# Decoder layer on one core: attention rounds written out, the first FFN weight units prepared earlier, the hand-over to the mixer rearranged

## What is computed

```python
x = x + attention(layernorm(x))      # 16 heads of 32, causal softmax, biases
x = x + mixer(ctx, ctx, layernorm(x))  # 32 heads of 8: all 8x8 products k_i * v_j along the
                                       # sequence, causally convolved with the head's kernel, + D,
                                       # then summed against q_i
x = x + ffn(layernorm(x))            # rows and weights rounded to int8 grids; gate and up of 1408
                                       # (w_gate_up: 2816 rows), silu(gate) * up, down to 512
```

## Time and profile before

| | us |
|---|---|
| median of 3 runs | 1222.92 (1220.35 to 1227.15) |
| the profiled execution | 1222.95 |
| its span | 1221.1 |
| PE busy | 1130.7 (93%) |
| DVE busy | 1002.1 (82%) |
| POOL busy | 945.4 (77%) |
| ACT busy | 878.4 (72%) |

### The profile page before, as it was taken

How to read it: one execution, slowest core, us unless ns; L and a number is a source line. 1 busy time by engine, 2 the same in 40 slices (tenths; PEclk the granted TensorE clock), 3 DMA queues, 4 the chain that set the end, 5 groups by cost and what they waited for, 6 DMA issues and landing times. The chain is left out here.

```text
span 1221.1 us, 31917 instructions
## 1 busy us (share of the span) xinstructions
PE 1130.7 (93%) x10114; PEld 814.0 (67%) x10114; DVE 1002.1 (82%) x3147; ACT 878.4 (72%) x1811; POOL 945.4 (77%) x1085
## 2 busy tenths in 40 slices
PE   7889999999999999998768899999999999999996
PEld 6777777878777787776446566666666666666662
DVE  5678888878787887887768788988889888898875
ACT  3878878878787887887746566667666676666764
POOL 0377787767778776877736799999999999999983
PEclk9989999999999999999679999999999999999999
DMA  6345655556555555566675433444434443344410
GB/s 213 101 165 183 187 169 159 186 168 194 181 167 169 166 174 185 180 207 191 235 230 190 146 105 129 137 147 137 115 127 137 148 137 114 129 137 148 134 32 26
DMA packets 88342, 188.84 MB, mean 155 GB/s; under 512 B 12351, under 2 KB 29017, under 8 KB 88089
## 3 DMA queue, kind: packets, MB, share of 16 engines
q1 hardware_dynamic: 87353, 186.74, 48.7%
q10 hardware_dynamic: 864, 0.66, 0.3%
HBM read 107.57 MB, written 54.62 MB: 133 GB/s over the span
## 5 line engine op out<-in xcount | busy, mean ns | idle before, releaser
L780 ACT ACTIVATE prob<-masked,negmax 128x128 f32<-128x128 f32 (+1 forms) x512 | 206.4, 454 | 73.6 <-DVE negmax L915 72.6
L915 DVE CUSTOM_DVE_ANT_0 masked<-s_ps,mask_f 128x128 f32<-128x128 f32 (+1 forms) x512 | 161.1, 352 | 29.7 <-PE s_ps L661 14.9
L1255 PE MATMUL f_ps<-wqkv,xiT 128*128 128x512 bf16 (+1 forms) x768 | 174.5, 364 | 2.4 <-DVE up L1712 1.5
L1538 POOL TENSOR_TENSOR tree<-prod 128x512 f32<-128x512 f32 x128 | 163.1, 1274 | 10.6 <-DVE prod L1642 10.4
L1446 ACT ACTIVATE silu<-gate,sx 128x512 f32<-128x512 f32 (+1 forms) x96 | 66.0, 687 | 136.1 <-DVE gate L1706 136.1
L539 POOL TENSOR_TENSOR kv_s<-kv_f,kv_s 128x1152 f16<-128x1152 f32 x64 | 152.3, 2379 | 4.6 <-ACT kv_s L794 4.6
L921 DVE TENSOR_TENSOR pT_lo<-t_ps,pT_hi 128x384 f16<-128x384 f32 x256 | 140.6, 550 | 15.4 <-ACT pT_hi L788 15.1
L532 POOL TENSOR_TENSOR kv_f<-c_in 128x1024 f32<-128x1024 f32 x64 | 146.0, 2281 | 0.2 <-DMA c_in<-in_ctxr 0.2
L788 ACT CAST pT_hi<-t_ps 128x384 f16<-128x384 f32 x256 | 122.2, 478 | 29.7 <-PE t_ps L670 28.5
L598 PE MATMUL g_ps<-x_all,wqkv 128*128 128x256 f16 x512 | 140.1, 274 | 3.1 <-DVE x_all L879 3.1
L599 PE MATMUL g_ps<-x_all,wqkv 128*128 128x256 f16 x512 | 140.1, 274 | 0.0
(11 more groups left out here) (187 smaller groups left out, 3591.9 us busy)
## 6 DMA issues: line engine op xcount, KB each, us to landing
kv_pairs<-kv_s SPq DMA_DIRECT2D x64, 576.0 KB, 3.4
kv<-kv_pairs SPq DMA_DIRECT2D x32, 1152.0 KB, 8.6
c_in<-in_ctxr SPq DMA_DIRECT2D x64, 192.0 KB, 2.5
q_st<-w_raw SPq DMA_DIRECT2D x192, 64.0 KB, 2.0
k_st<-w_raw SPq DMA_DIRECT2D x192, 64.0 KB, 2.0
x_all<-in_x SPq DMA_DIRECT2D x16, 512.0 KB, 6.6
x_res<-in_x SPq DMA_DIRECT2D x16, 512.0 KB, 6.1
x_after_attention<-x_out SPq DMA_DIRECT2D x16, 512.0 KB, 4.4
```

The lines of the kernel that those rows point to most:

```text
L780: ins = nc.scalar.activation(prob[h % 2][:, at:at + w], masked[h % 2][:, at:at + w], ACT.Exp, bias=negmax[:, h % 2, t:t + 1], scale=-1.0)
L915: ins = nc.vector.tensor_tensor_reduce(masked[h % 2][:, at:at + w], s_ps[h % 2][:, at:at + w], mask_f[:, S - w:S], -1.0, FAR, ALU.add, ALU ...
L1255: mm = nc.tensor.matmul(f_ps[side][:, 0:w], xiT[:, t, :], w1T[:, t, side * I_FF + at:side * I_FF + at + w], start=t == 0, stop=t == DT - 1)
L1538: nc.gpsimd.tensor_tensor(tree4[:], pr[:, :, 0:4 * w], pr[:, :, 4 * w:8 * w], ALU.add).then_inc(t4_done, 1)
```

## The change

All rounds of attention are written out: the `Fori` of each of the five engines becomes a Python loop, and the branches for register values go. Pair sets are numbered through (`q`), and their number per round comes from `pair_sets(i)`, which is 4 for all.

Units 0 to 3 are loaded at the end of SP's lists for rounds 8 and 9, their maxima found one half at a time in steps 3 and 6 of rounds 10 to 13 (one unit a round), their scales in step 7, the halves rounded in steps 8 and 11. Round 15 has no unit work. Units 4 and 5 are loaded in round 14, 6 and 7 early in round 15.

In round 15 POOL's list has a pair set, a low part and a value bias ahead of the residual's bias; ACT makes the high part of the set before at step 5 instead of 3. In the tail POOL adds the last residual's bias ahead of the last two low parts. PE turns the four halves of units 0 and 1 before the last "A" jobs, into banks that the heads leave free; ACT and DVE take two each. DVE handles units 4 and 5 before the first "O" job's end and unit 6 between the two. The last `x_out` is stored by halves of 128 tokens: the mixer's first loads need the first half alone.

At the mixer's start `FIRST` has six halves instead of ten, and DVE finds maxima and scales of all four units 7 to 10 after its first statistics, where it found those of 7 and 8 before them.

```diff
+UNIT_MAX = {(B - 6 + u, s): (u, k) for u in range(4) for s, k in ((3, 0), (6, 1))}
+UNIT_SCALES = {(r, s + 1): u for (r, s), (u, k) in UNIT_MAX.items() if k == 1}
+UNIT_SCALE = {(r, s + 2 + 3 * n): (u, n) for (r, s), (u, k) in UNIT_MAX.items() if k == 1 for n in range(2)}
...
+    def find_part(self, dve, u, k):
+
+        if k == 0:
+            dve.wait_ge(self.loaded[u], 16)
+        n = UNITS[u][1] + k
+        ins = self.nc.vector.tensor_reduce(self.maxima[:, n:n + 1], self.home(u)[:, k, :], AX_X, ALU.max, apply_absolute_value=True)
+        if k == 1:
+            ins.then_inc(self.max_done, 1)
...
+    def scale_part(self, act, u, k):
+
+        if k == 0:
+            act.wait_ge(self.inv_done, u + 1)
+        n, rows = UNITS[u][1] + k, self.home(u)[:, k, :]
+        ins = self.nc.scalar.activation(rows, rows, ACT.Copy, bias=MAGIC, scale=self.inv[:, n:n + 1])
+        if k == 1:
+            ins.then_inc(self.scaled, 1)
...
+                if i == B - 8:
 
                     sp.wait_ge(w_split, split_after(3))
                     W.load(sp, 0, w1)
                     W.load(sp, 1, w1)
-                if last:
+                if i == B - 7:
+                    W.load(sp, 2, w1)
+                    W.load(sp, 3, w1)
+                if i == B - 2:
 
                     for j in range(HPT):
                         sp.wait_ge(stacked[j], (B - 1) * (6 * 16))
                     W.load(sp, 4, w1)
                     W.load(sp, 5, w1)
...
-            with sp.Fori(LOOP0, LOOP1 - 1, 2) as i:
+            for i in range(LOOP0, LOOP1, 2):
                 body(i, 0)
                 body(i + 1, 1)
...
-            store_pairs(B - 1, 2)
-            store_pairs(B - 1, 3)
-            store(B - 1, jobs_before(B) + len(JOBS_END))
+            store_pairs(NQ - 2)
+            store_pairs(NQ - 1)
+            for m, done in ((0, x_stored), (1, x_last)):
+
+                sp.wait_ge(g_free, jobs_before(B) + 3 + m)
+                sp.dma_start(x1d[B - 1, m * P:(m + 1) * P, :], x_out[:, m, :]).then_inc(done, 16)
+            sp.wait_ge(early_taken, EARLY)
...
+                if last:
+
+                    pairs(q)
+                    pairs_low(q - 1)
+                    value_bias(i, p, 0)
+                    biased_residual()
+                    pairs(q + 1)
+                    pairs_low(q)
+                    value_bias(i, p, 1)
+                    pairs(q + 2)
+                    pairs_low(q + 1)
+                    value_bias(i, p, 2)
+                    pairs(q + 3)
+                    return
...
             value_bias(B - 1, 1, HPT - 1)
-            pairs_low(B - 1, 3)
             pool.wait_ge(res_loaded, B * 16)
             nc.gpsimd.tensor_tensor(x_res[:], x_res[:], bo_b[:, None, :].broadcast_to([P, TT, D]),
                                     ALU.add).then_inc(res_biased, 1)
+            pairs_low(NQ - 2)
+            pairs_low(NQ - 1)
...
+            pe.wait_ge(max_done, B * H)
+            pe.wait_ge(plo_done, B * H)
+            for k in range(EARLY):
+                W.turn_rows(pe, *early[k], early_bank[k], eye_f).then_inc(early_turned, 1)
...
-                if k == 2:
-                    for u in range(IN_ROUND, IN_TAIL):
-                        W.find_maxima(dve, u)
-                        W.find_scales(dve, u)
+                for u in {2: range(IN_ROUND, IN_TAIL - 1), 3: range(IN_TAIL - 1, IN_TAIL)}.get(k, ()):
+                    W.find_maxima(dve, u)
+                    W.find_scales(dve, u)
                 low(B, 0, n0 + k, j, g_ps[(n0 + k) % G], h0 + his(JOBS_END, k))
...
+    FIRST = HALVES[EARLY:10] + ["T"]
+    FIRST_BANK, FIRST_ACT = (0, 1, 2, 3, 4, 5, 0), (0, 2, 4)
...
-            for u in (7, 8):
-                W.find_maxima(dve, u)
-                W.find_scales(dve, u)
+            take(1)
+            take(3)
             ln_stats(0, 0)
             aggregate(0, st2, st2_done, mv2, mv2_done)
-            take(2)
-            take(4)
-            for u in (9, 10):
+            take(5)
+            for u in (7, 8, 9, 10):
                 W.find_maxima(dve, u)
                 W.find_scales(dve, u)
             take(6)
-            take(8)
-            take(10)
```

More of the change, by code:

```diff
@@ L550, in body, with biased_residual @@
             def body(i, p):
-                jobs = round_jobs(i)
-                first = isinstance(i, int) and i == 0
-                if has(jobs, "O"):
-                    value_bias(i - 1, 1 - p, HPT - 1)
+                jobs, n, q, last = round_jobs(i), pair_sets(i), pairs_before(i), i == B - 1
+                def biased_residual():
                     pool.wait_ge(res_loaded, i * 16)
@@ L732, in _ @@
                 body(i, i % 2)
-            with pe.Fori(LOOP0, LOOP1 - 1, 2) as i:
+            for i in range(LOOP0, LOOP1, 2):
                 body(i, 0)
@@ L854, in _ @@
                 prob_high((B - 1) * H + s - 2, s - 2)
-            pairs_high(B - 1, 3)
+            pairs_high(NQ - 1)
+            for k in range(0, EARLY, 2):
+                act.wait_ge(early_turned, k + 1)
+                u, b, nb = early[k]
+                nc.scalar.activation(W.target(u, b, nb), early_bank[k][:, 0:nb * P].rearrange("p (t c) -> p t c", t=nb), ACT.Copy,
+                                     bias=-MAGIC).then_inc(early_taken, 1)
             n0 = jobs_before(B)
```

205 lines of the change are left out of this document (113 added, 92 removed).

## The result

| | before | after |
|---|---|---|
| median, us | 1222.92 (7 runs, 1220.35 to 1227.15) | 1215.6 (7 runs, 1212.2 to 1219.7) |
| ratio | 1 | 0.9939, 95% 0.9920 to 0.9959 |
| profiled execution / span | 1222.95 / 1221.1 | 1219.47 / 1217.7 |

The change makes the kernel 0.6% faster, 7.3 us by the medians, where 12 had been forecast. A ratio interval that ends at 0.9959 excludes no change at all, but leaves the size open between 0.4% and 0.8%.

The account below looks back on a forecast made before the run. PE was taken to set a full round's length, with loop edges and round 15's mutual waits on top. From 1222.95 us, -9.2 + 2.4 + 0.5 - 7.5 + 0.5 + 1.2 = -12.1 gave 1211 us, range 1203 to 1220.

Parts of the forecast that it names:

- Loop edges: Even rounds after a loop edge: writing the loop out removes the edges, -9.2 us (bounds 0 and 9.2).
- Rival 5: Loop written out: the edges' time stays as fetch waits in straight-line code, 1220.2 us; chance 0.06.
- Units in rounds 10 to 13: Weight units 0 to 3 put into these rounds make PE late by +0.6 us a round, +2.4 in all.
- their loads: Unit loads ahead of the residual's load in rounds 8 and 9: POOL late but catches up, +0.5 us.
- a push on step 9: Rounds 10 to 13: second half maximum, small ops and step 8 rounding delay step 9's row maximum about 0.6 us, step 12 too.
- The rounding of step 11: Rounds 10 to 13, ScalarE: hidden behind steps where PE bounds; if that cover is gone, 0.66 us a round.
- Rival 3: Rounds 10 to 13, step 7: POOL's op blocks VectorE's small scaling, up to 2.1 us a round, 1219.4 us; chance 0.07.
- Round 15: Without unit work VectorE and ScalarE stop delaying each other: -7.5 us (bounds 2 to 11).
- Tail: Last value bias V to the mixer's first x load: POOL's reordered list takes what the halves give, +0.5 us (-2.5 to +3).
- the halves: Tail: storing the last x by halves frees the first x load from the second's landing, 1 to 2 us less.
- Mixer start: Four units behind the first statistics: +3.0 for units 7 and 8, less about 1.8 for evictions, +1.2 us.
- signs: Right: rounds 4-9 35.0, 10-13 35.3-36, round 15 28-31 us. Wrong: 2 us scaling in 10-13, round 15 above 34.

Follow-up runs that it names:

- unroll_only: The kernel before with its five loops written out and nothing else; 1214.69 us, ratio 0.9922.
- queue_order: Kernel after with loads of units 4 to 10 behind round 15's second pair store and its residual ahead of the x store; 1214.85 us, ratio 0.9893.
- all_four: All repairs on the kernel after: units 0-3 spread over rounds 6-14, weights requeued, earlier maxima, low parts first, scalings by column, unit 6 later; 1200.68 us, ratio 0.9795.
- maxima_first: Kernel after with maxima and scales of units 7 and 8 ahead of the mixer's first evictions and statistics on VectorE; 1214.45 us, ratio 0.9899.
- loads_behind: Kernel after with the loads of units 0 to 3 behind the residual's load on SyncE's queue instead of ahead; 1213.11 us, ratio 0.9897.

## Why the prediction was right, and where its sum was not

The direction was right and the time (1215.6) lies in the range of 1203 to 1220, just outside the forecast's own 1207 to 1215; the forecast of 1211 was 4.6 us too low. It was right by the loop alone: all other terms were forecast at -2.9 in sum, and against the kernel with the loop alone their stages come to +0.8. Their errors go both ways (units and loads 4.9 too cheap, the tail 2.1 too dear), and that these partly cancel is luck.

From profile to profile, up to the products, the stages are: rounds 0 and 1 -0.9 (not forecast; +0.8 with the loop alone, so not an effect that can be relied on), rounds 2 to 13 -1.7, round 15 to V -5.4, V to x load -1.6, from there to the statistics +0.2, statistics to products +1.4, together -8.0.

- **Loop edges, -9.2.** Right: -9.4 with the loop alone, and the "issue" waits that remain, 0.9 us at most, are hidden. Rival 5 is out: no round keeps the edge's time.
- **Units in rounds 10 to 13, +2.4, and their loads, +0.5.** These are the terms that failed: +7.8 against the loop alone. The working priced the second half maximum by a push on step 9 that would reach step 12. That push isn't there: steps 9 and 12 kept their 2.02 and 1.61 us. What it missed was nearer: the divide of step 7, on the same engine and in the same step, for which the values waited (+0.44). The rounding of step 11, called hidden, cost 0.54; its named fallback, 0.66 if that cover is gone, was the better figure. Together 1.1 a round, 4.5 in all.
- The loads: "POOL works 26.8 of 35 us, so it catches up" was true of POOL, but not of what meets a late POOL: 1.5 us by lateness itself and 1.9 by the blocked scaling in round 10 (1.2 and 2.1 by the estimate above). Round 9 paid next to nothing (35.10). Rival 3 had mechanism and price right (2.07 us, the 2.1 forecast) and the number of places wrong: one round of four in the kernel after, since it takes a late POOL to bring them together. It deserved to be a part of the loads' term, not a separate case.
- **Round 15, -7.5.** -5.4 from profile to profile up to V, -4.7 from first to last scores, -7.8 against unroll_only, of which about 2 are that run's own held-up scaling. The mechanism was as stated (the maxima's wait 8.2 to 1.9). The prediction counted the small scaling's 3.8 us as work and didn't see that 3.1 us of it were the wait of its rival 3, met already in the kernel before. What was not seen is that ScalarE's wait for its pair buffer, 3.7 us, would follow from the weights on the queue ahead of a store; in the kernel before it was 2.2 us up to V, a row that the prediction didn't read. In the two kernels without it (queue_order, all_four) the gain is 9.7 to 9.8.
- **Tail, +0.5.** -1.6 measured. The chain named there (residual, bias, low parts, last pair store, x halves) is what the runs show, 10.6 us from the bias; it was sized 0.8 us too dear behind the bias (V + 4 to V + 15.4 is 11.4), and the bias began at V + 2.7, not V + 4. That the halves give 1 to 2 was too much: 0.66.
- **Mixer start, +1.2.** +1.4 measured, and +2.1 against unroll_only; maxima_first takes 3.0 off, the forecast's own 3.0 for units 7 and 8.

What was written as signs came out as: rounds 4 to 9 at 34.9 to 35.2 and no "issue" wait of 2.4 us (right), rounds 11 to 13 at 36.06, just above the 36 given, round 10 outside, round 15 at 32.1 from first to last scores where 28 to 31 stood, the last pair store at V + 9.8 where "after 10 us" stood. A scaling of 2 us in rounds 10 to 13, a sign of being wrong, was there once.

## What to carry to other kernels

Work moved off a crowded stage fits elsewhere only in pieces that are no larger than one idle gap of the engine that gets it: list, step by step, which instruction stands behind it on that engine and who waits for that one. A load that is added to a queue is paid by what stands behind it there, so put transfers with a long due time behind the short-dated ones of the same place. And a change whose parts cancel hides both: the loop alone gave all of this one's gain, and the rest of it, rearranged after each part had been measured by itself, became worth another 1.3% (0.9795 against 0.9922).

## What the runs showed of the hardware

- A small VectorE scaling on 128x2 f32 that begins inside a GpSimd op lasts until that op ends (2.07, 2.08, 2.35 us beside ops on 128x1024 or 128x1152, 0.39 beside one on 128x128). In the thirteen profiles it did so with more than 0.17 us of the op left 44 times, and ended 0.02 to 0.03 us behind the op every time; with no GpSimd op running it took 0.16 to 0.17. On 128x1 it took 0.14 to 0.16 in all 40 such meetings, and the reciprocal on 128x2 0.17, so it isn't stopped either.
- 1 MB of weights issued ahead of the residual's load moved the bias that waits for it by 5.9 us (from 10.0 us after round 10's first scores in loads_behind, 398.82, to 15.9 in the kernel after, 402.06), in a round in which the DMA engines were busy 0.62 of the time: the order of issue counted, not the mean load.
- The mixer's last 50 us took 49.8 to 54.4 us in the profiles of thirteen kernels that have the same code there, with a granted clock of 0.99 (all_four, 50.6 us window) to 0.90 (after). What decides it was not tried.
